# Two linear-attention layers: queries and y turned by block transposes and transfers in place of TensorE, y one step later

## What is computed

```python
xn = layernorm(x)
q, k, v = xn @ Wq + bq, xn @ Wk + bk, (xn @ Wv + bv) * valid
q = softmax(q, axis=features of a head)        # per token
k = softmax(k + mask, axis=tokens)             # per feature
att = einsum('bnhd,bnhl->bhdl', k, v)
y   = einsum('bnhd,bhdl->bnhl', q, att)
h = silu(layernorm(y) * (1 + scale) + shift)   # scale, shift = silu(emb) @ W_emb + b_emb
x = x + h @ Wout + bout
```

## Time and profile before

| | |
|---|---|
| median of 3 runs | 937.99 us (936.15 to 938.22) |
| profiled execution, whole time | 937.17 us |
| its span in the trace | 935.4 us |
| PE busy | 900.6 us, 96% of the span |
| DVE busy | 728.3 us, 78% |
| ACT busy | 591.0 us, 63% |
| POOL busy | 441.6 us, 47% |

### The profile page before, as it was taken

The page is one execution under the profiler, slowest core; times in us unless marked ns, Lnnn a source line. Parts: engine busy times, 40 slices in busy tenths (PEclk is TensorE's granted clock), DMA queues, the critical chain, the costliest instruction groups (busy, mean ns, idle before and its releaser), DMA issues.

```text
span 935.4 us, 20347 instructions
## 1 busy us (share of the span) xinstructions
PE 900.6 (96%) x7069; PEld 768.2 (82%) x7069; DVE 728.3 (78%) x1350; ACT 591.0 (63%) x1445; POOL 441.6 (47%) x621
## 2 busy tenths in 40 slices
PE   5799999999999999999989999999999999999986
PEld 4678888888888888888878888888888888888864
DVE  6867787878787887878877888887778888777664
ACT  5466575675676667667776666567567666655544
POOL 2454454444554455445655555445445545443321
PEclk9999999999999999999989999999999999999999
DMA  9655353523423222222443233323223322323120
GB/s 295 248 190 164 119 163 114 165 74 119 119 97 97 80 74 77 79 80 97 142 124 119 95 110 119 111 88 96 94 88 120 118 98 87 101 85 108 68 69 34
DMA packets 70011, 105.86 MB, mean 113 GB/s; under 512 B 6782, under 2 KB 46838, under 8 KB 69910
## 3 DMA queue, kind: packets, MB, share of 16 engines
q1 hardware_dynamic: 68832, 103.05, 33.3%
q10 hardware_dynamic: 1078, 1.50, 0.7%
HBM read 63.63 MB, written 40.89 MB: 112 GB/s over the span
## 4 chain that ended last, share of the span: by engine, by line
PE 87%; DVE 4%; DMA 3%; ACT 3%; issue 2%; POOL 1%; SPq 0%; ACTq 0%; DVEq 0%; POOLq 0%
PE PS L698 71%; PE PS L781 6%; PE PS L765 3%; PE PS L739 3%; PE PS L747 3%; DMA k_turned<-KT 1%; DMA EK<-k_turned 1%; PE PS L818 1%; ACT Z L549 1%; ACT SK L529 1%; SPq L331 0%; DVE BNX L910 0%; DMA X<-in_x 0%; DVE KT L978 0%; ACT YN L535 0%
## 5 line engine op out<-in xcount | busy, mean ns | idle before, releaser
L535 ACT ACTIVATE YN<-YN,NBY,RSY 128x512 f32<-128x512 f32 x64 | 52.2, 815 | 252.4 <-POOL NBY L435 252.3
L698 PE MATMUL PS<-XH,WH_k 128*128 128x256 f32 x512 | 146.0, 285 | 3.9 <-DVE WL_k L266 3.9
L698 PE MATMUL PS<-XH,WL_k 128*128 128x256 f32 x512 | 145.9, 285 | 0.0
L698 PE MATMUL PS<-XL,WH_k 128*128 128x256 f32 x512 | 145.8, 285 | 0.0
L409 POOL TENSOR_SCALAR VEY<-MVY 128x1 f32<-128x1 f32 x64 | 14.5, 226 | 233.1 <-DVE MVY L1032 232.7
L454 POOL TENSOR_TENSOR SQ<-SQ,QM 128x512 f32<-128x512 f32 x64 | 67.0, 1047 | 103.0 <-DVE QM L993 102.9
L698 PE MATMUL PS<-WH_o,HH 128*128 128x512 f32 x256 | 107.6, 420 | 1.9 <-ACT HH L581 1.6
L698 PE MATMUL PS<-WH_v,XH 128*128 128x512 f32 x256 | 106.4, 415 | 0.5 <-DVE WL_v L266 0.5
L698 PE MATMUL PS<-WH_q,XH 128*128 128x512 f32 x256 | 106.9, 417 | 0.0
L698 PEld LDWEIGHTS PS<-XH,WH_k 128*128 128x128 f32 x512 | 99.1, 194 | 7.2 <-issue 4.2
L529 ACT ACTIVATE SK<-SK,KN 128x128 f32<-128x128 f32 x256 | 98.9, 387 | 5.3 <-DVE KN L962 5.3
(11 more groups left out here) (126 smaller groups left out, 2192.5 us busy)
## 6 DMA issues: line engine op xcount, KB each, us to landing
k_turned<-KT SPq DMA_DIRECT2D x32, 512.0 KB, 2.6
EK<-k_turned SPq DMA_DIRECT2D x128, 128.0 KB, 2.8
x_turned<-XS SPq DMA_DIRECT2D x30, 512.0 KB, 2.6
XT<-x_turned SPq DMA_DIRECT2D x120, 128.0 KB, 2.8
out_x<-X SPq DMA_DIRECT2D x32, 256.0 KB, 2.4
X<-in_x SPq DMA_DIRECT2D x9, 512.0 KB, 5.6
X<-in_film SPq DMA_DIRECT2D x2, 2048.0 KB, 17.0
STAGE<-in_film SPq DMA_DIRECT2D x4, 1024.0 KB, 7.4
```

The lines of the kernel that those rows point to most:

```text
L535: eng.activation(YN[:, :], YN[:, :], ACT.Identity, bias=NBY[:, :], scale=RSY[:, :]).then_inc(act_yn, 1)
L698: mm = eng.matmul(dst, left[a](c), right[b](c), start=(c == 0 and a + b == 0), stop=(c == C - 1 and a == 1))
```

## The change

- `turn_queries` and `turn_y` move from PE to DVE: one 32x32 block transpose of 128x512 each, into the two halves of a new tile QS. For each slot SP writes QS to a new DRAM buffer qy_turned (`write_qy`, 512 KB) and reads it back in four transfers into QT (`read_qy`). ACT's `exp_q` and `film` read QT in place of PSUM. Only the last two tiles' queries and the last four tiles' y are still turned on PE.
- Film, h and output come one slot later (tile s-4 in place of s-3).
- `normalise_keys` (its multiplication) and `h_low` (but for the last four tiles) move from DVE to GpSimd; DVE keeps the reciprocal (`key_sums`).
- SQ and the lower buffer of x (XF) have one copy in place of two; values and output have a PSUM bank each.
- On PE, a slot's order becomes keys, values, queries, attention, output, mix. The orders of a slot on DVE, ACT, POOL and SP are rewritten too. The loop has 63 slots in place of 64, and the drain is written out anew. The loads and splits of the second layer's weights are reordered.

SP's queue:

```diff
+            def write_qy(s):
+                eng.wait_ge(dve_qs, s)
+                if s >= 3:
+                    eng.wait_ge(dve_ys, s - 2)
+                n = 2 if s >= 3 else 1
+                eng.dma_start(QD[s % 2, :, :, 0:n, :], QS[:, :, 0:n, :, :].rearrange("p q h c n -> p q (h c n)"))\
+                   .then_inc(st_qd[s % 2], 16)
+            def read_qy(s):
+                wait_written(eng, s)
+                if s == 1:
+                    eng.wait_ge(dve_xl, 2 * FIRST)
+                else:
+                    eng.wait_ge(act_eq, s - 1)
+                if s >= 4:
+                    eng.wait_ge(act_z, s - 3)
...
+                for fq in range(Q):
+                    eng.dma_start(QT[32 * fq:32 * fq + 32, :, 0:n, :, :].rearrange("p q h c n -> p q (h c n)"), src[fq])\
+                       .then_inc(ld_qt[s % 2], 16)
...
-            for s in range(1, NT):
-                if s >= B + 4:
-                    store(s - B - 4)
+            for s in range(1, NT - 1):
+                if s == B:
+                    load_second(eng, 6)
                 if s % 2 == 0 and s + 2 < NT:
                     eng.wait_ge(dve_ka, s)
                     load_mask(eng, s // 2 + 1)
-                for g in block_turn_at(s) if s > 1 else []:
-                    place_x(g)
+                if s > 1:
+                    for g in x_pair_at(s):
+                        write_x(g)
+                write_qy(s)
+                if s > 1:
+                    for g in x_pair_at(s):
+                        read_x(g)
+                read_qy(s)
+                if s == B - 1:
+                    load_second(eng, 5)
```

ACT's `exp_q` and `film`, and the head of its slot:

```diff
             def exp_q(j):
-                eng.wait_ge(pe_tq, j + 1)
+                if j < LAST_Q:
+                    wait_placed(eng, j + 1)
+                    src = QT[:, :, 0, :, :].rearrange("p q c n -> p c q n")
...
             def film(o):
-                eng.wait_ge(pe_ty, o + 1)
+                if o < LAST_Y:
+                    wait_placed(eng, o + 3)
...
             for s in SLOTS:
-                i, j, o, m = s, s - 2, s - 3, s + 2
+                i, j, o, m = s, s - 2, s - 4, s + 2
                 if 0 <= o:
-                    norm_y(o)
+                    film(o)
+                if s >= 3:
+                    norm_y(s - 3)
+                if 0 <= o:
+                    h_high(o)
```

The slot and the drain of PE:

```diff
             for s in SLOTS:
...
-                if 0 <= j:
-                    turn_queries(j)
-                if 0 <= o:
-                    turn_y(o)
                 values(i)
...
+                if s != B:
+                    queries(i)
                 if 0 <= j:
                     attention(j)
...
+                if 0 <= o:
+                    output(o)
                 if 0 <= j:
                     mix(j)
-                if 0 <= o:
-                    output(o)
                 if s == B:
                     queries(i)
+            values(t2)
+            turn_queries(t1)
+            queries(t2)
+            attention(t0)
+            turn_y(t9)
+            output(LAST_Y - 1)
+            mix(t0)
+            attention(t1)
+            turn_queries(t2)
+            output(t9)
+            mix(t1)
+            attention(t2)
+            turn_y(t0)
+            mix(t2)
+            output(t0)
+            turn_y(t1)
+            output(t1)
+            turn_y(t2)
+            output(t2)
```

469 lines of the change are left out of this document (281 added, 188 removed).

## The result

| | before | after |
|---|---|---|
| median | 938.11 us (936.15 to 938.24) | 974.39 us (969.18 to 981.22, 4 runs) |
| profiled execution, span | 935.4 us | 979.4 us |
| PE busy | 900.6 | 873.1 |
| DVE, ACT, POOL busy | 728.3, 591.0, 441.6 | 674.4, 609.8, 555.9 |

A forecast was written before the change was run, and what follows sets the result against it. PE, busy 96% of the span, was taken to bound the kernel: 937.2 - 53 (PE work) + 3 (ring) - 1 (start) + 1 (layer change) + 1 (drain) = 888 us; range 878 to 906 for 8 in 10.

The forecast's parts named there:

- 0.87: PE in the loop: time saved per slot by dropping turns and a group switch, shortening 13.52 us to 12.65.
- the price put on GpSimd holding the port: DVE's multiplication of h: a full GpSimd operation, 1.3 us, if the port rule holds; without the rule 0.
- So I put 0.05 us a slot, 3 us in all, on this ring: Loop allowance for late queries and y transfers through DRAM, with ends of 0 and 0.4 us a slot.
- the ring: Loop chain film, h, turns, write, reads, next film: 11.6 us, 12.0 when x is turned, against a 12.65 us slot.
- the sign that I set for a failure: Loop: the forecast fails if reads of QT land later than some 4.5 us into the next slot.
- The sentence on reads "in front": SP's queue in slots turning x: x's four reads, 1.7 us of issuing, precede queries and y, making 12.0 us.
- Longer queueing is what I can't bound from these rows: DMA traffic: room on average at 57% load, but longer queueing was left without a bound.
- the 2.65 of the sum: Write of queries and y until SP can issue the read: 2.65 us in the 11.6 us chain.
- The rival "slower than before: transfers lengthen": Loop: write plus read at least 1.8 us longer per average slot; at 2.2 us longer, 966 us; chance 0.06.
- +1, with -4 and +3 as ends: Layer change, slots 31 to 33: 7 to 9 us of excess again, against 7.1 before, so 1 us added.
- +1, ends -3 and +3: Drain from the mix of slot 62: 44 to 45 us, against 43.6 before, so 1 us added.
- lie bare: Drain: last y turned only after the preceding output, exposing its film, tanh and split; within the +1 us.

The follow-up runs named there:

- e11: Changed kernel with x's four reads on SP's queue moved between the keys' write and the keys' reads; 952.86 us, ratio 1.0167.
- e3: Changed kernel with the keys' write put in front of the reads of queries and y on SP's queue; 994.34 us, ratio 1.0597.
- e1: Changed kernel with the second layer's output bias load issued before the write of slot 31; 967.37 us, ratio 1.0329.
- e6: Changed kernel with POOL's output bias addition back at the end of its slot, the load left in place; 969.3 us, ratio 1.0359.
- the best version: Changed kernel with x's reads in the keys' gap, early bias load, earlier drain turns of y, conditioning copy into EQ; 932.24 us, ratio 0.9956.
- e2: Changed kernel with each of the last two turns of y in the drain put before the preceding output; 960.07 us, ratio 1.0229.
- e5: Changed kernel with the conditioning sums' copy in slots 6, 9, 12, 15 put into EQ right behind the film; 968.36 us, ratio 1.0334.
- e4: Changed kernel with the multiplication of the key scaling moved back from POOL to DVE; 974.09 us, ratio 1.0411.

## Why the prediction was wrong

**Right.** PE loses 0.91 us a slot, for 0.87: slots without a wait take 12.62 us in layer 0 (13.53 before) and 12.82 in layer 1 (13.73 before), for 12.65. DVE fell to 674.4 / 64 = 10.5 us a slot (10.9 said), POOL rose to 8.7 (9.2 said). The multiplication of h takes 693 ns on average, so the price put on GpSimd holding the port is 0 here. By the rule of the Trainium skill (SBUF — State Buffer, section "SBUF: two separate sides") it could have been up to 1.3 us. This instruction is no test of it: in 61 of 62 cases no large GpSimd operation ran beside it, and the one beside which one did took 849 ns. The key scaling of the kernel before is a test, and there the trace agrees: it took 693 ns on average in the 9 tiles without a large GpSimd operation beside it, and 1346 in the 55 with one.

**The step that failed: "So I put 0.05 us a slot, 3 us in all, on this ring".** I took the ring of film, h, turns, write and read for the only chain that the new transfers lengthen. It is late too (ACT waits 182.4 us for QT), but in the changed kernel PE seldom feels it: 6.9 us of waits in front of its matmuls are put down to issue. What PE waits for is EK, 31.0 us, and with the clock behind the longer waits more. The keys' chain had no term at all, and the sign that I set for a failure (reads of QT too late) watches the other chain. The sentence on reads "in front" counted x's reads against queries and y, and stopped there; the queue goes on, and the keys' write and reads stand last on it. The trace before had what was needed: the keys landed 2.0 us before attention, a slot was to get 0.9 us shorter, and the reads of queries and y were to be put between x's reads and the keys' write, so that eight reads, 3.5 us of issuing, stand there in one run. With the start from the trace after (turn ends 391.34, SP free at 392.30) and the spread of the rows that I had (write to read 2.65 to 5.03, reads 1.3 + 2.4 to 4.4), EK comes between 398.7 and 403.1, for an attention due at 400.87: PE waits in part of these slots. The edit e11, which changes only the order of this chain, gives 21.5 us.

**The transfers.** "Longer queueing is what I can't bound from these rows" was true, and it was left out of the range nevertheless. The keys' write to read went from 2.64 to 4.35 us. The write of queries and y lets the queue go on after 2.71 us in the slots that also turn x, near the 2.65 of the sum, and after 3.75 in the others, where the keys' four reads stand in front of it. So the ring is longer than its sum too, and e3 shows that it has no room. The load matters by place: the average share of 53% was forecast well, as 57. The Trainium skill's range for HBM access (DMA: Bandwidth & Descriptors, section "Latency and other measured facts": 0.2 us on average, 2 us at high load) has room for it: the keys' write is 1.7 longer with 1 MB of reads in front. No run here tells that latency from queueing behind these reads. The rival "slower than before: transfers lengthen" had the right sign, but another chain, and that its time (966) is near is in part luck: it put 81 us into the loop, where slots 17 to 30 and 33 to 62 lie 37 us above the forecast, and the rest of the loss has other causes.

**Layer change: "+1, with -4 and +3 as ends".** It was +13.7, or 15.3 above the forecast. Here 4.5 (e1) to 5.7 us (e6) of the stage are POOL's addition at the head of its slot behind a late load. I had stepped through the weights' chunks and not through the bias loads, which stand behind the keys on SP's queue. Some 10 us stay in the best version. The largest wait left there is one of 6.9 us for EQ in slot 32: ACT's split of the query weights waits 4.91 us for a load that SP issues at 468.57, behind the keys' write (459.29) and their reads (465.79). This is read from the trace, not tested.

**Drain: "+1, ends -3 and +3".** It was +15.0. The prediction says that film, tanh and split of the last y "lie bare", and prices it at 1 us. It is so for the last two: they are two waits of 4.4 us, and behind each an output runs at the lower clock. e2 gives 13.0 of the 15 us of this stage back.

**Slots 2 to 17** had no term. The conditioning copy shares Z with the film (6.0 us by e5). In slot 3 PE waits 6.6 us for EQ (6.8 in the best version), and the granted clock is 0.80 to 0.82 in the windows from 66 to 93 us; slots 3 and 4 are 16.4 and 17.7 us long. e4 is the one test of this part: it takes away DVE's wait for the scaling in slot 3, and slot 4 gives the gain back. In the best version slots 3 and 4 are 10.6 us above a slot shortened as the others are, and slots 9 and 15, where PE still waits 3.8 and 2.0 us for the copy behind a late QT, 8.7 us. What makes slots 3 and 4 long I have read but not settled.

**What stays open.** The best version is 44 us above 888: 21.7 in slots 2 to 17, 11.1 in slots 33 to 62 (the EK waits left), 10.0 at the layer change and 1 to 2 in each of the others. A tile of its own for the conditioning sums wasn't tried, nor was x's route moved to the slots without keys. With the four edits 42 of the 86 us between forecast and result are accounted for.

## What to carry to other kernels

When a change adds transfers to a queue, write out the chain of every transfer that stands behind them until its user, not only the new data's own, and read its slack before: the keys had 2.0 us of it, the change used it up and gave back nearly all that it saved. On a queue whose owner waits for a write, put into that wait the reads that are not urgent: here it was worth 21.5 us for a few lines moved, while x's write and reads on a second queue cost 67. And price a bare wait on TensorE with the slower clock behind it: in one case 2.1 us of waiting cost 3.6, and shortening two waits of 4.4 in the drain gave 13.

## What was not expected of the hardware

- A write of 512 KB took 2.64 us until its queue could go on (median of 25), 4.35 with 1 MB of reads issued in front of it on the same queue, 3.76 with nearly all of x's half of those bytes left out (and with x's write shorter too), and 6.15 with x's half issued from another engine's queue. Reads issued right behind it on its own queue left it at 4.13.
- The granted clock fell to 0.54 over the 3 us behind a wait of 2.1 us, and to 0.50 in 480 to 492 us, where PE waited for the value weights for 12.0.
- The landing of the four reads of EK hardly moved, 2.5 to 3.9 us with a median of 2.8, as before; it is the write that took the load.
- On DVE the key scaling of the kernel before, one shape, took 693 ns on average with no large GpSimd operation beside it and 1346 with one (9 and 55 of 64); the longest took 1751.
